# A decoder layer's second half: two of its three activation transposes moved from TensorE to DMA

## What is computed

```python
q    = x1 @ W_tgt.T + b_tgt                     # 8 heads of 64
k, v = split((ctx @ W_src.T + b_src) * mask)
attn = softmax(where(mask == 0, -inf, q @ k.T / 8))
o    = attn @ v                                  # attention output, 512 x 512
x2   = layernorm(x1 + concat([x1, o]) @ W_out.T + b_out)
y    = layernorm(x2 + ffn(x2))                   # 512 -> 2048 -> 512, hidden layer in fp8
```

## Time and profile before

| | before |
|---|---|
| three runs, median | 1962.86 us |
| the profiled execution | 1961.34 us |
| its span | 1959.5 us |
| TensorE busy in the span | 1845.5 us (94%) |
| VectorE, ScalarE, GpSimd busy | 68%, 40%, 27% |
| mean granted clock of TensorE | 0.982 |
| start of the second half | 839 us |

### The profile page before, as it was taken

How to read it: one execution, slowest core, us unless ns; L and a number is a source line. 1 busy time by engine, 2 the same in 40 slices (tenths; PEclk the granted TensorE clock), 3 DMA queues, 4 the chain that set the end, 5 groups by cost and what they waited for, 6 DMA issues and landing times. The chain is left out here.

```text
span 1959.5 us, 33372 instructions
## 1 busy us (share of the span) xinstructions
PE 1845.5 (94%) x12588; PEld 1016.1 (52%) x12588; DVE 1333.6 (68%) x1698; ACT 787.2 (40%) x1209; POOL 522.3 (27%) x546
## 2 busy tenths in 40 slices
PE   5999999999989999868999999999999999999988
PEld 4565555645544665445545455455454554544543
DVE  3588999899879989767565564655655556556521
ACT  3422222222222222247465363562653644626522
POOL 1334864585448326600000001001001000010010
PEclk8999999999999999989999999999999999999999
DMA  6545347425643456565313304104123041041000
GB/s 227 113 119 116 81 116 167 118 71 140 146 108 80 126 141 154 149 141 178 73 42 58 100 1 103 55 1 109 48 46 99 14 103 55 1 104 33 12 33 22
DMA packets 290831, 176.60 MB, mean 90 GB/s; under 512 B 194793, under 2 KB 248041, under 8 KB 290690
## 3 DMA queue, kind: packets, MB, share of 16 engines
q1 hardware_dynamic: 286320, 174.17, 35.6%
q10 hardware_dynamic: 4370, 0.34, 0.2%
HBM read 94.75 MB, written 33.55 MB: 65 GB/s over the span
## 5 line engine op out<-in xcount | busy, mean ns | idle before, releaser
L1362 DVE TENSOR_TENSOR p_lo<-k,p_hi 128x1024 f16<-128x1024 f32 x128 | 156.8, 1225 | 193.8 <-ACT p_hi L1250 193.8
L81 POOL TENSOR_TENSOR vsb<-mvb,consts 128x1 f32<-128x1 f32 x64 | 12.1, 189 | 1029.4 <-DVE mvb L1377 1029.4
L1051 PE MATMUL b_ff<-x2T_hi,w1T_hi 128*128 128x512 f16 x512 | 195.0, 381 | 2.3 <-DVE x2T_lo L1362 2.3
L1407 DVE CUSTOM_DVE_ANT_0 junk<-b_sx,mneg 128x512 f16<-128x512 f32 x256 | 176.1, 688 | 30.6 <-issue 22.2
L1051 PE MATMUL b_ff<-x2T_lo,w1T_hi 128*128 128x512 f16 x512 | 195.0, 381 | 0.0
L1051 PE MATMUL b_ff<-x2T_hi,w1T_lo 128*128 128x512 f16 x512 | 194.8, 380 | 0.0
L1282 ACT ACTIVATE k<-b_st,mbias 128x512 f32<-128x512 f32 x256 | 161.8, 685 | 14.1 <-PE b_st L1095 14.1
L1250 ACT ACTIVATE p_hi<-k 128x1024 f16<-128x1024 f32 x128 | 135.3, 1057 | 44.1 <-PE b_av L1110 41.7
L745 DVE TENSOR_TENSOR prod<-q,k 128x4096 f32<-128x4096 f32 x32 | 143.2, 4476 | 13.0 <-ACT q L677 12.1
L1274 ACT ACTIVATE hq<-b_ff,b 128x512 fp8e4<-128x512 f32 x128 | 88.0, 687 | 155.9 <-PE b_ff L1051 149.2
L595 PE MATMUL pj_b<-winT_hi,xT_hi 128*128 128x512 f16 x384 | 146.3, 381 | 3.9 <-DMA xT_lo<-rows_lo 3.9
(11 more groups left out here) (258 smaller groups left out, 4332.6 us busy)
## 6 DMA issues: line engine op xcount, KB each, us to landing
cn<-in_ctx_dram SPq DMA_DIRECT2D x64, 256.0 KB, 3.1
k<-kT_scratch SPq DMA_DIRECT2D x24, 512.0 KB, 7.8
xn<-in_x_dram SPq DMA_DIRECT2D x32, 256.0 KB, 3.0
x<-in_x_dram SPq DMA_DIRECT2D x32, 256.0 KB, 3.2
x_scratch<-x SPq DMA_DIRECT2D x32, 256.0 KB, 2.2
q<-x_scratch SPq DMA_DIRECT2D x8, 1024.0 KB, 5.6
q<-x_scratch SPq DMA_DIRECT2D x32, 256.0 KB, 4.1
out_dram<-q SPq DMA_DIRECT2D x32, 256.0 KB, 4.3
```

The lines of the kernel that those rows point to most:

```text
L1051: mm = pe.matmul(out, a, c, start=(start and n == 0), stop=end)
L1362: dve.tensor_tensor(dst, bank, hi, ALU.subtract).then_inc(out, 1)
L1407: dve.tensor_tensor_reduce(junk[:, :], sx_b[tt % 2][:, :], mneg[:, :], 1.0, NEG, ALU.add, ALU.max, mx[:, h % 2, tt:tt + 1]).then_inc(s["sx ...
```

## The change

x1 and `o` are no longer turned by TensorE. ScalarE writes the hi part of a tile's rows into `row_hi[tt]` (four buffers, shared by `o` and x1; `output_hi`, `x1_hi`), GpSimd writes the lo part over the first half of the source rows (`o_lo`, `x1_lo`; `output_lo`, `x1_rows_lo`), and SP turns both with two DMAs per tile (`turn_output`, `turn_x1`). That is sixteen turning DMAs per batch. A tile of `o` waits until x1 of the same buffer has been turned, a tile of x1 until `o` has. x1 of the next batch is turned only when `output_x1` has read the tile of the batch before (`x1_used`). `load_heads` becomes `load_keys` and `load_values`. TensorE waits for each tile of `oT` in `output_rest`, and for all four tiles of `x1T` before the first query product. x2 is turned as before. Before the loop, x1 of batch 0 is the first thing on SP's list of the second half, and the turns of `o` of batch 0 and x1 of batch 1 follow the values of batch 1.

```diff
+    row_hi = [sb(f"row_hi{i}", [P, E], F16) for i in range(4)]
+    o_lo, x1_lo = ([z[:, tt, :].bitcast(F16)[:, 0:E] for tt in range(4)] for z in (o, x1n))
...
         @block.sync
+            def turn_output(b, tt):
+                sp.wait_ge(s["o_row_lo"], 4 * b + tt + 1)
+                stand_alone(sp, alone["sp"])
+                for dst, rows in ((oT[0], row_hi[tt][:, :]), (oT[1], o_lo[tt])):
+                    sp.dma_start_transpose(col(dst, tt), rows).then_inc(o_turned[tt], 16)
+
+            def turn_x1(b, tt, first=False):
+                sp.wait_ge(s["x1_row_lo"], 4 * b + tt + 1)
+                stand_alone(sp, alone["sp"])
+                if not first:
+                    sp.wait_ge(s["x1_used"], 4 * (b - 1) + tt + 1)
+                    stand_alone(sp, alone["sp"])
+                for dst, rows in ((x1T[0], row_hi[tt][:, :]), (x1T[1], x1_lo[tt])):
+                    sp.dma_start_transpose(col(dst, tt), rows).then_inc(x1_turned[tt], 16)
...
+            for tt in range(4):
+                turn_x1(0, tt, True)
             all_stored(sp, w)
-            load_heads(0, True)
+            load_keys(0, True)
+            load_values(0, True)
...
-            load_heads(1, False)
+            load_keys(1, False)
+            load_values(1, False)
+            for tt in range(4):
+                turn_output(0, tt)
+            for tt in range(4):
+                turn_x1(1, tt)
             with sp.Fori(0, NBATCH - 2) as b:
                 for g in range(len(GROUPS)):
                     queries(b + 1, g)
                 load_x1(b + 2)
-                load_heads(b + 2, False)
+                load_keys(b + 2, False)
+                load_values(b + 2, False)
                 for tt in range(4):
+                    if tt < 2:
+                        store(b, tt)
+                    turn_output(b + 1, tt)
+                for tt in range(2):
+                    load_residual(b + 1, tt, False)
+                for tt in range(2, 4):
                     store(b, tt)
                 for tt in range(4):
-                    load_residual(b + 1, tt, False)
+                    turn_x1(b + 2, tt)
+                    if tt in (1, 2):
+                        load_residual(b + 1, tt + 1, False)
...
         @block.gpsimd
+            def output_lo(b, tt):
+                pool.wait_ge(s["o_row_hi"], 4 * b + tt + 1)
+                stand_alone(pool, alone["act"])
+                pool.tensor_tensor(o_lo[tt], o[:, tt, :], row_hi[tt][:, :], ALU.subtract).then_inc(s["o_row_lo"], 1)
...
         @block.tensor
             def queries(b, i, part=slice(None)):
                 if i == 0:
-                    pe.wait_ge(s["xt_lo"], 4 * b + 4)
+                    for tt in range(4):
+                        pe.wait_ge(x1_turned[tt], 32 * (b + 1))
+                        stand_alone(pe, alone["pe"])
...
-                pe.wait_ge(s["o_norm"], 8 * b + 8)
-                for tt in range(4):
-                    transposes(tq_b[tt], o[:, tt, :], s["ot_filled"])
...
             def output_rest(b):
-                pe.wait_ge(s["ot_lo"], 4 * b + 4)
                 for tt in range(4):
+                    pe.wait_ge(o_turned[tt], 32 * (b + 1))
+                    stand_alone(pe, alone["pe"])
...
             with pe.Fori(0, NBATCH - 1) as b:
-                x1_transposes(b + 1, False)
                 output_rest(b)
                 queries_and_first_scores(b + 1, b)
                 heads(b + 1, b)
...
         @block.scalar
-            def x1_hi(b):
+            def x1_hi(b, first=False):
+                if first:
+                    for i in range(3):
+                        act.wait_ge(w.x1_out[i], 16 * len(range(i, NB * T, 3)))
+                act.wait_ge(w.x_ld, 16 * (b + 1))
+                stand_alone(act, alone["act"])
                 for tt in range(4):
-                    hi(col(x1T[0], tt), bank4(tq_b[tt]), s["xt_filled"], 4 * b + tt + 1, s["xt_hi"])
+                    if not first:
+                        act.wait_ge(o_turned[tt], 32 * b)
+                        stand_alone(act, alone["act"])
+                    act.activation(row_hi[tt][:, :], x1n[:, tt, :], ACT.Copy).then_inc(s["x1_row_hi"], 1)
...
             for n, (_, high, _) in enumerate(jobs):
+                if n == 2:
+                    x1_hi(0, True)
                 hi(high, bank4(om_b[n % 4]), s["wq_filled"], n + 1, s["wq_hi"], WS)
-            x1_hi(0)
```

More of the change, by code:

```diff
@@ L1018, in _ @@
             for tt in range(4):
+                if tt < 2:
+                    store(last - 1, tt)
+                turn_output(last, tt)
+            for tt in range(2):
+                load_residual(last, tt, False)
+            for tt in range(2, 4):
                 store(last - 1, tt)
-            for tt in range(4):
+            for tt in range(2, 4):
                 load_residual(last, tt, False)
@@ L1032, in _, with norm_factors @@
             pool.memset(rows_b[:, :], 0.0).then_inc(s["made"], 1)
[L1033 to L1038, removed]
+            def norm_factors(l, b, tt):
+                pool.wait_ge(s[l + "_mv"], 4 * b + tt + 1)
+                i = tt + (4 if l == "l3" else 0)
+                layer_norm_factors(pool, w, mv[i], vs, rstd[i], s[l + "_rstd"], 4 * (4 * b + tt))
@@ new lines, in _ @@
+            for tt in range(4):
+                x1_rows_lo(0, tt)
+            for tt in range(4):
+                output_lo(0, tt)
+            for tt in range(4):
+                x1_rows_lo(1, tt)
+            with pool.Fori(0, NBATCH - 2) as b:
+                for tt in range(4):
+                    norm_factors("l2", b, tt)
+                for tt in range(2):
+                    norm_factors("l3", b, tt)
+                output_lo(b + 1, 0)
+                output_lo(b + 1, 1)
+                for tt in range(2, 4):
+                    output_lo(b + 1, tt)
+                    norm_factors("l3", b, tt)
+                for tt in range(4):
+                    x1_rows_lo(b + 2, tt)
@@ new lines, in _ @@
+            last = NBATCH - 1
+            for tt in range(4):
+                norm_factors("l2", last - 1, tt)
+            for tt in range(2):
+                norm_factors("l3", last - 1, tt)
+            output_lo(last, 0)
+            output_lo(last, 1)
+            for tt in range(2, 4):
+                output_lo(last, tt)
+                norm_factors("l3", last - 1, tt)
+            for l in ("l2", "l3"):
+                for tt in range(4):
+                    norm_factors(l, last, tt)
@@ L1045, in transposes, with products @@
                 mm.then_inc(done, 1)
-            def products(out, operands, bias, done, start=True):
+            def products(out, operands, bias, done, start=True, stop=True):
                 for n, (a, c) in enumerate(operands):
-                    end = bias is None and done is not None and n == len(operands) - 1
+                    end = stop and bias is None and done is not None and n == len(operands) - 1
                     mm = pe.matmul(out, a, c, start=(start and n == 0), stop=end)
@@ L1521, in _ @@
                 masks(b + 1)
-                x1_low(b + 1)
                 for tt in range(4):
```

34 lines of the change are left out of this document (19 added, 15 removed).

## The result

The changed kernel takes **2034.29 us** (median of four runs, 2029.88 to 2038.42) against 1963.72 for the kernel before on the same chip: a ratio of 1.0368 over the runs (the two medians alone give 1.0359), 95% interval 1.0345 to 1.0391. It is slower by 70.6 us, where 49 were forecast. The profiled execution took 2030.94 us, its span is 2029.1.

A forecast was written before the change was run, and what follows sets the result against it. TensorE, busy 94% of the span, was taken as the bound. Loop 27.6 + first boundary 13.25 + start 9.9 - end 1.75 = 49.0 us, added to 1961.3, gave 2010 us; range 1983 to 2042, 8 in 10.

The forecast's parts named there:

- What bounds, and the mechanism: Second half: TensorE, busy 94% of the span, bounds; SP's new list ends late, so TensorE waits for the turns.
- What comes off TensorE: Transposes of output and x1 at each batch boundary: 1.75 + 1.79 = 3.54 us saved, all on the path.
- What goes on SP, in the six boundaries of its loop: Turns, plain DMAs, gap and waits behind the value loads: 26.2 us of SP, so TensorE waits 6.4 us for x1.
- What the wait does to the clock: After each wait TensorE runs partly at the lower clock: 1.7 us more per wait, bounds 0 and 1.7.
- The start: Start of the second half: x1 turns ahead on SP delay query copies; first scores 9.9 us late, bounds 5.7 to 11.4.
- The first boundary: Batch 0 to 1: pairs stand alone on SP; queries 11.55 us late, + 1.7 for the clock: 13.25 (11 to 14.5).
- The second wait: First boundary, TensorE before the queries: expected idle of 6 us or more, after 5 or more before the output product.
- The end: End of batch 7: only the output's transposes come off TensorE, saving 1.75 us.
- Rivals 1 and 2: Turns hidden in the loop, paid at edges: 1961.5 us, chance 0.07; turns as short as plain DMAs: 1947 us, 0.09.
- Rival 3: Turns queue behind the value loads, one long issue per boundary, 4.3 x 7 = 30 us more: 2040 us, chance 0.12.
- the rule that the prediction names: Trainium skill: on TRN2 transposing DMAs are as fast as regular ones; the prediction read it for transfer, not SP's issue.

The follow-up runs named there:

- own_rows: Changed kernel with four row buffers of their own for x1, so its split need not wait for the output's turns; 2035.5 us.
- output_only: Half of the change: attention output turned by DMA, x1 turned by TensorE as in the kernel before; 1963.7 us, ratio 1.0003 to 1.0032.
- x1_only: Other half of the change: x1 turned by DMA, attention output turned by TensorE as in the kernel before; 1968.9 us, ratio 1.0027 to 1.0057.
- both_best: Changed kernel with own x1 buffers, reordered start, late value loads, plain DMAs on ScalarE, first output product split, first-boundary x1 turned before output; 1961.1 us.
- values_late: Changed kernel with the next batch's value loads moved from ahead of the turns to behind the first two groups of query copies; 2009.2 us.
- output_best: Kernel turning only the output by DMA, with late value loads, first output product split, TensorE's added loop wait removed; 1942.1 us, second run 1946.2.
- start_order: Changed kernel with SP's list reordered at the second half's start: keys and first weights ahead of x1 turns, first query copies earlier; 2029.8 us.

## Why the prediction was right, and which term was too small

**What bounds, and the mechanism: right.** The releasers are DMAs into `x1T_lo`, `oT_lo` and the query copies, never ScalarE or GpSimd; own_rows leaves the split out, output_only and x1_only show that the number of turns on the list decides.

**"What comes off TensorE", 3.54 us: right in size.** both_best gains 2.8 of it per turn with 0.8 of wait left.

**"What goes on SP, in the six boundaries of its loop": the term that was mis-sized.** Forecast 26.2 us from the end of `v_lo` to the end of the list; measured 28.2 to 28.7. In the boundary shown it is 1126.10 - 1097.49 = 28.6: the sixteen turning issues add up to 21.3 us (forecast 20.3: it took the pair of the earlier trace rows for all, and two output turns here took 1.67 and 2.18), and the plain DMAs (3.5) and the gaps between issues (3.8), in which the register waits lie, to 7.3 (forecast 5.9). TensorE was also ready sooner, 1117.47 - 1097.49 = 20.0 us after `v_lo` instead of 21.0, mostly because the value loads now took 7.8 us and not 7.16. So the wait is 9.4 on average and not 6.4.

**"What the wait does to the clock", 1.7 us: right in kind, 1.9 measured.** 8.0 us more per turn is 9.4 - 3.54 + 2.1; nine matmuls at 0.43 instead of 0.216 are 1.9 of the 2.1. Six turns: 47.9 us against 27.6 forecast, and 8.0 is the upper bound that the text gave. These 20.3 us are the miss (69.6 against 49.0); what the other terms were off cancels (start +2.1, end +2.5, first boundary -2.0, the shorter first half -2.3).

**The start, 9.9: too small, and hidden by luck.** By the span's clock the first scores came 876.99 - 867.34 = 9.65 us late, as forecast. Counted from the first transposes they came 39.97 - 28.02 = 11.95 us late, above the bound of 11.4; the first half happened to be 2.3 us shorter. The term that was short is the landing of the query copies: the third was issued at 872.07, and TensorE went on 4.9 us later, where the text had 2.0.

**The first boundary, 13.25: right in size.** Up to the first query of batch 1 the text has 11.55; its 1.7 for the clock comes after that query. From the first scores to that query it is 111.2 us instead of 99.95, 11.3 more. The rows there are the ones forecast, against the earlier trace rows:

```profile
964.64 0.92 SPq L970 DMA_DIRECT2D v_lo<-v_scratch  x1
...
985.59 1.27 SPq L948 DMA_TRANSPOSE x1T_lo<-q  x1
```

```profile
970.75 0.58 PE L1134 MATMUL b_sx<-wxT_hi,oT_hi 128*128 128x512 f16 x1 [11.27 <-DMA oT_lo<-k]
...
988.22 0.59 PE L1134 MATMUL b_st<-x1T_hi,wtT_hi 128*128 128x512 f16 x1 [4.34 <-DMA x1T_lo<-q]
```

The second wait is 4.3 us and not "6 or more": the output product began 5.2 us after `v_lo`, where the text has 3.7, and took 13.1 us instead of 11.2, with matmuls at twice the spacing behind its own wait. That time came off the wait of the queries.

**The end, -1.75: +0.7 instead**, since the stretch holds the lower clock behind the last wait.

**The rivals.** Rivals 1 and 2 fell: no turn was shorter than 1.19 us. Rival 3 has a part of the truth: single output turns took up to 2.2 us behind the value loads (up to 2.3 in values_late, without them), though nowhere 4.3 more per boundary. Read for the issue, the rule that the prediction names, a turning DMA as fast as a regular one, does not hold: the median of 28 output turns into `oT_lo` is 1.26 us, that of the 128 KB value loads in output_best 0.64.

## What to carry to other kernels

Moving work from a busy engine to DMA moves it to a list that one engine issues in order; add up the issue time of that list between what releases its first entry and what its last entry is wanted for, with the loads that stand ahead of it, before counting what the busy engine saves. Here half of the move fits into the gap and, with the loads put behind it, is worth 0.7 to 0.9% (the moved loads alone, without turns, were not measured), while all of it costs 3.7%. The edges of a loop need their own sum: there the cover is shorter, and they took back all that both_best won.

## What the hardware showed that was not expected

- The same four value loads hold SP for 7.3 to 8.5 us at the end of a batch and for about 3 us behind the query copies. The issues in the loop of the changed kernel, then of output_best (ns, min/median/max):

```profile
L968 SPq DMA_DIRECT2D v_hi<-v_scratch x24: 542/845/5722, 1088.7 to 1794.8; - x24
```

```profile
L968 SPq DMA_DIRECT2D v_hi<-v_scratch x24: 542/636/1147, 1104.6 to 1752.6; - x24
```

  The mean share of the DMA engines is 1.15 in the first place (1088.75 to 1096.67) and 0.64 in the second (1104.5 to 1108). That an issue is short while the engines have room fits these numbers, but is only argued.
- TensorE's idle time at the loop's start, 0.7 us a turn before, is 0.5 us in six turns of values_late, against 3.7 in the changed kernel with the same program of TensorE. It is not a matter of the value loads alone: both_best, which has them late as well, keeps 3.4. The traces hold a candidate: in every loop turn, 16 KB on a DMA queue of instructions (q8) land shortly before TensorE's first matmul. Where TensorE sat idle by more than 0.3 us without a named cause, the matmul came 1.5 to 1.9 us after that landing (1.9 to 2.1 in output_only, with its added wait). So it may wait for its own instructions, whose landing other transfers delay; this is argued from the times, and no run tests it.
- A turn's issue was longer where plain transfers were in flight. The four pairs at the start of the second half took at most 1.35 us an issue in the changed kernel, where they stand alone (mean share of the DMA engines 0.44, 844 to 855), and up to 3.81 in start_order, behind keys and weights (share 1.22, 842 to 852).
